# One bank table for eight PSUM banks, and a new order of steps, in a fused attention and transformer kernel

## The chip, the cores and the metric

The kernel is one program on one core of a Trainium2 chip. The metric is the device time of one execution in microseconds (us); less is better. Engines are named as in the profile: PE is TensorE (PEld its weight loads), DVE is VectorE, ACT is ScalarE, POOL is GpSimd and SP is SyncE, which here issues DMAs alone.

## The reference, cut to what matters

The input is x of shape 4 x 512 x 128 in float32. It goes through a small attention block and then through a six-layer transformer, each between layer norms and with a residual.

```python
x = x + layernorm(attention(layernorm(x)))        # 16 heads of 8, causal, rope, gelu on q and k
t = layernorm(x)
for i in range(6):                                # DEPTH
    s = shift_tokens(t)                           # features 64..127 moved down one token
    q, k, v = split(s @ Wqkv[i])                  # 16 heads of 64
    q, k = rotary(l2norm(q) * qs), rotary(l2norm(k) * ks)
    p = softmax(8 * q @ k.T)                      # windows of 32 tokens: own and previous
    t = (p @ v) @ Wo[i] + t
    s = shift_tokens(t)
    a, g = split((layernorm(s) * ln_g + ln_b) @ W1[i] + b1[i])
    t = (a * gelu(g)) @ W2[i] + b2[i] + t            # 341 hidden features
x = x + layernorm(t)
```

## The kernel before

There are two large stages. The first is the small attention block: 16 groups of four heads, each group 16 score steps that share four slots of two PSUM banks (`a_ring`) in turn. The loop of DVE there takes eight row maxima a group (L676), brings the output of the group two before into shape (`normalise`, L664 and L666, which reads a slot that PE wrote at L934), and adds the maxima to the queries (L682). PE waits for a slot until its last reader is done, so it waits for `normalise` before a later score step (L906) may write that slot.

The second stage is the transformer. A unit u is one layer of one of the four sequences, so there are 24 units. A unit is cut into steps, and each engine has a hand-kept table of steps (`TENSOR_STEPS`, `VECTOR_STEPS`, `SCALAR_STEPS`, `GPSIMD_STEPS`). A row (kind, n, lag) stands for step n of that kind of unit pass minus lag. `unrolled` runs the table once for each pass, so that in one pass an engine works on three or four units that are at different places. All engines execute in order; they meet by semaphores, one for each kind of step. The steps of a unit, with their lines:

- project 0 to 15: PE multiplies by one 128-column slice of Wk or Wq (L1003). DVE multiplies the result by cos and sin (rotate, L756), ACT squares it for the norms (L556). SP swaps neighbouring partitions by two DMAs (L428) and POOL adds the two halves (add, L490). The buffer between rotate and add has four slots, so rotate n waits for add n-4.
- sums 0 to 3: PE sums the squares (L1013), ACT copies the sums (nevac, L562), PE turns them (nturn, L1024), DVE takes inverse roots by Newton steps (newton, L768 and L712 to L723; for the keys also a split in three bf16 parts, L740 to L746).
- nback and spread: PE turns the keys' roots back (L1029), ACT copies them (nrows, L566), PE spreads them over the partitions (L1037), DVE multiplies the keys (keyed, L777).
- score 0 to 3: PE (L1056), mask and max on DVE (L781, L785), lower and scale on POOL (L494, L500), exp on ACT (L573), psum on DVE (L788, L790), pnorm on POOL (L504), flip on DVE (L794).
- xturn, mix and out: PE turns x (L1045), mixes it by the probabilities (L1072), ACT copies (zcopy, L578), PE multiplies by Wv Wo (out, L1080, made by the step vo at L980 once a layer) and ACT copies the sum (x1, L584 and L585).
- mean, var, rows, hid 0 to 2 and down: the feed-forward part on PE (L1090, L1096, L1101, L1110 and L1113, L1117), with center, xsq, bias, gelu and new on ACT and rstd, gain and gated on DVE.

PSUM has eight banks of 512 floats. In this stage they are three fixed groups: `ps_r` (two banks) for project, mean, var, rows, hid and down; `ps_s` (two) for sums 0 and 1, nturn 0, nback, spread, score and vo; `ps_z` (four) for mix, out, xturn, sums 2 and 3 and nturn 1. So project n takes the bank of project n-2 and waits until ACT has squared it, and score n waits until DVE has masked score n-1. Weights of the feed-forward part are loaded by SP in the middle of its swaps (`load_ffn`).

## Time and profile before

| what | value |
|---|---|
| device time, three runs | 2112.12, 2115.53, 2119.7 us; median 2115.53 |
| profiled execution, span from first to last instruction | 2110.2 us |
| busy: PE, DVE, POOL, ACT | 1875.9, 1560.5, 1102.0, 913.3 us |
| chain that ended last, by engine | PE 67%, DVE 21%, POOL 4%, waits of no known cause 3% |

The runs carry no split of time around the span; for the profiled execution the span is all that is known, and the median of the runs is 5.3 us longer. "Busy" of PE is modelled from the ends of matmuls, so its idle time is what is left between them. "Idle before" in a row is how long the engine had stood still ahead of that instruction, and the name behind the arrow is the instruction that released it. The mean time of one instruction on DVE in the page's table of groups is 1214 ns for the rotate at L756, 1220 for L781, 1211 for L785, 1209 for L788 and 1223 for L794.

### The profile page before, as it was taken

How to read it: one execution, taken by the hardware profiler on the slowest of the kernel's cores; microseconds unless marked ns; L12 is line 12 of the kernel's file. 1: busy time of each engine (PE TensorE's matmuls, PEld its weight loads, DVE VectorE, ACT ScalarE, POOL GpSimd, SP SyncE). 2: the span in 40 equal slices, each digit the busy share in tenths (PEclk: the TensorE clock that was granted, in tenths of full speed). 3: DMA queues.
4: the chain of work that ended last, by engine and by line, in shares of the span. 5: the costliest groups of instructions: out<-in, count | busy, mean ns of one | idle time of the engine just before them, and what ended most of it. 6: DMA issues, size and time to landing. Idle time of an engine off the chain costs nothing.

```text
span 2110.2 us, 47076 instructions
## 1 busy us (share of the span) xinstructions
PE 1875.9 (89%) x20040; PEld 812.5 (39%) x20040; DVE 1560.5 (74%) x2524; ACT 913.3 (43%) x1460; POOL 1102.0 (52%) x822
## 2 busy tenths in 40 slices
PE   5999956799999999999999999999999998999974
PEld 2333423344334433444344344333443344344421
DVE  5555557877887788778877877888778878787823
ACT  1344422334454444445444544444444444544531
POOL 2122213765576557655755675567546755675520
PEclk9899987889999999999999999999999999999987
DMA  2200001121311132112212212131113211221100
GB/s 57 81 12 11 1 1 72 69 79 49 115 71 47 53 104 93 64 52 76 94 54 86 81 61 74 59 120 61 49 54 110 86 57 62 80 72 46 57 0 20
DMA packets 91750, 131.42 MB, mean 62 GB/s; under 512 B 16242, under 2 KB 35856, under 8 KB 91536
## 3 DMA queue, kind: packets, MB, share of 16 engines
q1 hardware_dynamic: 91540, 128.41, 17.6%
q8 instruction: 157, 2.57, 0.5%
q14 instruction: 53, 0.43, 0.1%
HBM read 24.54 MB, written 1.05 MB: 12 GB/s over the span
## 4 chain that ended last, share of the span: by engine, by line
PE 67%; DVE 21%; POOL 4%; issue 3%; ACT 2%; DMA 2%; SPq 0%; POOLq 0%; DVEq 0%; ACTq 0%
PE ps_z L1080 15%; PE ps_r L1003 11%; PE ps_s L1056 7%; DVE t L756 6%; PE ps_r L1110 4%; PE ps_z L1072 3%; PE ps_r L1117 3%; PE ps_r L1113 3%; PE ps_z L1013 2%; DVE t L676 2%; POOL k_hat L490 2%; DVE n_tmp L718 2%; PE ps_z L888 2%; DVE rnorm L723 2%; DVE n_tmp L720 2%
## 5 line engine op out<-in xcount | busy, mean ns | idle before, releaser
L756 DVE TENSOR_TENSOR t<-ps_r,rot 128x1024 f32<-128x1024 f32 x384 | 457.8, 1214 | 143.2 <-PE ps_r L1003 136.6
L1003 PE MATMUL ps_r<-xs,w_qk_sb 128*128 128x512 f32 x768 | 436.0, 673 | 41.0 <-ACT sq L556 40.5
L556 ACT ACTIVATE sq<-ps_r 128x512 f32<-128x512 f32 x384 | 229.6, 598 | 353.0 <-DVE t L756 350.7
L490 POOL TENSOR_TENSOR q_hat<-t 128x512 f32<-128x512 f32 x192 | 241.9, 1272 | 210.8 <-DMA t<-t 210.3
L1080 PE MATMUL ps_z<-z,vo 128*128 128x512 f32 x768 | 350.1, 599 | 0.0
L494 POOL TENSOR_TENSOR prob<-prob,top 128x1024 f32<-128x1024 f32 x96 | 182.5, 1901 | 280.2 <-DVE top L785 280.1
L490 POOL TENSOR_TENSOR k_hat<-t 128x512 f32<-128x512 f32 x192 | 242.3, 1276 | 86.4 <-DMA t<-t 86.3
L1003 PEld LDWEIGHTS ps_r<-xs,w_qk_sb 128*128 128x128 f32 x768 | 130.7, 200 | 293.9 <-ACT sq L556 173.4
L504 POOL TENSOR_TENSOR prob<-prob,sinv 128x1024 f32<-128x1024 f32 x96 | 185.9, 1936 | 90.5 <-DVE sinv L790 90.5
L578 ACT ACTIVATE z<-ps_z 128x512 f32<-128x512 f32 x384 | 208.1, 603 | 36.1 <-PE ps_z L1072 35.9
L1080 PEld LDWEIGHTS ps_z<-z,vo 128*128 128x128 f32 x768 | 144.6, 191 | 180.0 <-issue 179.9
L1072 PE MATMUL ps_z<-pt,xtk 32*128 32x512 f32 x1536 | 196.9, 628 | 7.8 <-ACT z L578 6.5
L500 POOL TENSOR_TENSOR prob<-prob,rnorm 128x1024 f32<-128x1024 f32 x96 | 182.6, 1902 | 7.5 <-POOL prob L494 0.4
L480 POOL TENSOR_SCALAR_AFFINE_SELECT t<-t 128x256 f32<-128x256 f32 x128 | 51.9, 406 | 217.8 <-ACT t L535 217.6
L1056 PE MATMUL ps_s<-k_hat,q_hat 64*32 64x64 f32 x12288 | 151.5, 228 | 14.3 <-DVE prob L781 7.8
L1056 PEld LDWEIGHTS ps_s<-k_hat,q_hat 64*32 64x32 f32 x12288 | 131.2, 106 | 75.4 <-DVE prob L781 43.6
L781 DVE TENSOR_TENSOR prob<-ps_s,band 128x1024 f32<-128x1024 f32 x96 | 117.1, 1220 | 54.5 <-PE ps_s L1056 54.4
L777 DVE TENSOR_TENSOR k_hat<-k_hat,ps_s 128x1024 f32<-128x1024 f32 x96 | 116.5, 1213 | 30.6 <-PE ps_s L1037 30.6
L608 ACT ACTIVATE gate<-ps_r,vec 128x512 f32<-128x512 f32 (+1 forms) x72 | 49.4, 685 | 206.1 <-PE ps_r L1110 205.8
L788 DVE TENSOR_REDUCE sinv<-prob 128x16 f32<-128x1024 f32 x96 | 116.1, 1209 | 10.6 <-ACT prob L573 10.6
L794 DVE STREAM_TRANSPOSE pt<-prob 128x1024 f32<-128x1024 f32 x96 | 117.4, 1223 | 8.1 <-POOL prob L504 4.6
L1072 PEld LDWEIGHTS ps_z<-pt,xtk 32*128 32x128 f32 x1536 | 70.5, 187 | 127.2 <-ACT z L578 58.8
(188 smaller groups left out, 2560.4 us busy)
## 6 DMA issues: line engine op xcount, KB each, us to landing
t<-t SPq DMA_DIRECT2D x768, 128.0 KB, 2.0
rot<-in_dram SPq DMA_DIRECT2D x12, 512.0 KB, 4.8
w_qk_sb<-in_dram SPq DMA_DIRECT2D x24, 256.0 KB, 3.3
w_vt_sb<-in_dram SPq DMA_DIRECT2D x6, 512.0 KB, 4.7
w_o_sb<-in_dram SPq DMA_DIRECT2D x6, 512.0 KB, 5.8
z<-q_hat SPq DMA_DIRECT2D x128, 16.0 KB
w_sb<-in_dram SPq DMA_DIRECT2D x6, 341.0 KB
x_tok<-in_dram SPq DMA_DIRECT2D x4, 256.0 KB, 3.6
```

Of the source, the lines that this page charges most:

```text
L490: nc.gpsimd.tensor_tensor(dst, t12[:, slot, 0, :], t2[:, slot, :], ALU.add).then_inc(added.sem, 1)
L494: nc.gpsimd.tensor_tensor(s, s, top[:, (TT * u + n) % P_SLOTS, :].unsqueeze(2).to_broadcast([P, HEADS, 2 * WIN]), ALU.subtract).then_inc(l ...
L500: nc.gpsimd.tensor_tensor(s, s, by.unsqueeze(2).to_broadcast([P, HEADS, 2 * WIN]), ALU.mult).then_inc(scaled.sem, 1)
L504: nc.gpsimd.tensor_tensor(s, s, sinv[:, (TT * u + n) % P_SLOTS, :].unsqueeze(2).to_broadcast([P, HEADS, 2 * WIN]), ALU.mult).then_inc(p_no ...
L556: nc.scalar.activation(sq[:, n % SQ_SLOTS, :], ps_r[n % 2][:, :], ACT.Square).then_inc(squared.sem, 1)
L578: nc.scalar.activation(z[:, :, at:at + WIN], ps_z[:, w, :].rearrange("p (h n) -> p h n", n=WIN), ACT.Copy).then_inc(z_copied.sem, 1)
L756: nc.vector.tensor_tensor(t12[:, slot, :, :], ps_r[n % 2][:, :].unsqueeze(1).to_broadcast([P, 2, SEQ]), rot[:, n // PAIRS, :, :], ALU.mult ...
L794: nc.vector.transpose(pt[:, n % 2, :, :, :].rearrange("p h a n -> p (h a n)"), prob[:, (TT * u + n) % P_SLOTS, :, :, :].rearrange("p c e n ...
L1003: nc.tensor.matmul(ps_r[n % 2][:, :], w_qk_sb[:, n, :], xs[:, seq, WIN:WIN + SEQ], start=True, stop=True).then_inc(projected.sem, 1)
L1056: ins = nc.tensor.matmul(ps_s[WIN * w:WIN * (w + 1), e, 2 * WIN * c:2 * WIN * (c + 1)], q_hat[rows, pair_at(c), at:at + WIN], k_hat[rows, ...
L1072: ins = nc.tensor.matmul(ps_z[:, w, :], xtk[rows, a, n, :], pt[rows, n % 2, :, a, :], start=(a == 0), stop=(a == 1), skip_group_check=True)
L1080: ins = nc.tensor.matmul(ps_z[:, 0, :], vo[:, h, :], z[:, h, :], start=(h == 0), stop=False, skip_group_check=True)
```

## The change

Four things change.

1. All eight banks are one tensor `ps`. A table `BANKS` gives each step of a unit its bank or banks. A pass over PE's plan notes for each use of a bank who held it last (`before`), and `vacant` makes PE wait, ahead of the first matmul that writes a bank, for the reader of that last tenant. The old waits that stood for the fixed groups go.
2. All four tables of steps have another order and other lags. The passes are cut at another place; relative to project, the steps of a unit on PE have the same lag as before, but for xturn, out 0, mean and var, whose lag behind project is one pass less.
3. `load_ffn` is issued by ACT, right after the last new of a layer, and not by SP.
4. In the first stage, DVE's `normalise` stands ahead of the sixth maximum of a group and not behind it.

```diff
+BANKS = {
+    "project": [(1,), (3,), (7,), (2,), (5,), (3,), (1,), (2,), (7,), (0,), (5,), (1,), (4,), (0,), (3,), (5,)],
+    "score": [(0, 1), (5, 6), (2, 3), (0, 1)],
+    "mix": [(4, 3, 7, 6), (4, 0, 2, 3), (7, 4, 6, 0), (1, 5, 3, 2)],
...
-        ps_rr = ctx.enter_context(nc.psum_tensor("ps_r", [P, 2, 512], F32))
-        ps_s = ctx.enter_context(nc.psum_tensor("ps_s", [P, 2, 512], F32))
-        ps_z = ctx.enter_context(nc.psum_tensor("ps_z", [P, 4, 512], F32))
+        ps = ctx.enter_context(nc.psum_tensor("ps", [P, 8, 512], F32))
...
+        before, tenant = {}, {at: ("vo", 0, -1) for at in banks("vo")}
+        for kind, n, u in plan_pe:
...
+                        before[what, n // per, u, k] = tenant.get(at)
+                        tenant[at] = (what, n // per, u, k)
...
+            def vacant(what, n, u):
+                for k in range(len(banks(what, n))):
+                    held = before[what, n, u, k]
...
+                    if kind == "project":
+                        pe.wait_ge(squared.sem, squared.at(v, m))
...
+                    elif kind == "nturn":
+                        pe.wait_ge(n_newton.sem, n_newton.done(newton_at[v, m], 0))
...
                 if kind == "project":
...
-                    if n >= 2:
-                        pe.wait_ge(squared.sem, squared.at(u, n - 2))
-                    else:
-                        pe.wait_ge(squared.sem, squared.at(u - 1, 14 + n))
...
-                    nc.tensor.matmul(ps_r[n % 2][:, :], w_qk_sb[:, n, :], xs[:, seq, WIN:WIN + SEQ], start=True, stop=True).then_inc(projected.sem, 1)
+                    vacant("project", n, u)
+                    nc.tensor.matmul(ps[:, banks("project", n)[0], :], w_qk_sb[:, n, :], xs[:, seq, WIN:WIN + SEQ], start=True, stop=True).then_inc(projected.sem, 1)
...
-                if seq == 2 and c == 2 and layer:
-                    sp.wait_ge(x_new.sem, x_new.done(layer * BATCH - 1))
-                    load_ffn(layer)
...
+                    if seq == BATCH - 1 and layer + 1 < DEPTH:
+                        act.wait_ge(x_new.sem, x_new.done(u))
+                        load_ffn(layer + 1)
...
             for i in range(GROUPS + 2):
                 for n in range(A_STEPS):
+                    if n == OUT_AFTER + 1 and i >= 2:
+                        normalise(i - 2)
...
-                    if n == OUT_AFTER + 1 and i >= 2:
-                        normalise(i - 2)
```

Of the tables of steps the rows themselves are shown as they come out. On PE, in the middle of the transformer stage before the change, from nturn 0 (`ident,nsb`) over the mixes (`pt,xtk`) to nback (`ident_bf,rk_pad`) and the first spread (`rk_rows,sel_rows_bf`):

```order
L1024 MATMUL ps_s<-ident,nsb 128x128 x4
L1003 MATMUL ps_r<-xs,w_qk_sb 128x512
L1072 MATMUL ps_z<-pt,xtk 128x512 x8
L1003 MATMUL ps_r<-xs,w_qk_sb 128x512 x2
L1072 MATMUL ps_z<-pt,xtk 128x512 x8
L1029 MATMUL ps_s<-ident_bf,rk_pad 128x128 x4
L1037 MATMUL ps_s<-rk_rows,sel_rows_bf 128x512 x2
```

And now the same stretch, with the same right-hand names:

```order
L1086 MATMUL ps<-ident,nsb 128x128 x4
L1150 MATMUL ps<-x1s,centre_w 128x512
L1129 MATMUL ps<-pt,xtk 128x512 x16
L1107 MATMUL ps<-ident,xs 128x128 x4
L1072 MATMUL ps<-xs,w_qk_sb 128x512
L1107 MATMUL ps<-ident,xs 128x128 x4
L1072 MATMUL ps<-xs,w_qk_sb 128x512
L1092 MATMUL ps<-ident_bf,rk_pad 128x128 x4
L1072 MATMUL ps<-xs,w_qk_sb 128x512 x2
L1155 MATMUL ps<-mean_w,xsq 128x1 x4
L1139 MATMUL ps<-z,vo 128x512 x4
L1099 MATMUL ps<-rk_rows,sel_rows_bf 128x512 x4
```

Between nturn 0 and nback there stand now mean, mix 2 and 3, both xturn and two projects, where there stood three projects and two mixes; between nback and spread, where nothing stood, there are now two projects, var and out 0.

On ACT, in the middle of the transformer stage now, from the copies x1 (`x1s`) over the square of project 8 and the last exp of a unit (`prob`) to the copies of mix (`z`):

```order
L611 ACTIVATE x1s<-ps 64x512
L612 ACTIVATE x1s<-ps 64x512
L584 ACTIVATE sq<-ps 128x512
L599 ACTIVATE prob<-prob 128x1024
L588 ACTIVATE nsb<-ps 128x512
L605 ACTIVATE z<-ps 128x16x32 x2
```

The last exp of a unit stands now behind x1, which waits for out 3; before, x1 was earlier and the exp stood behind the copies of mix 0.

## Rows read from the trace of the kernel before

**Rows 1.** Page: busy us (share of the span) xinstructions.

```profile
PE 1875.9 (89%) x20040; PEld 812.5 (39%) x20040; DVE 1560.5 (74%) x2524; ACT 913.3 (43%) x1460; POOL 1102.0 (52%) x822
```

**Rows 2.** Stretches: length, busy us (instructions) by engine, granted clock, DMA share, GB/s.

```profile
118.00:281.00 163.00, 148.29 (x1409) 64.99 (x1407) 86.47 (x128) 72.20 (x105) 37.75 (x93) 0.95 0.04 8
329.00:518.00 189.00, 159.32 (x2051) 70.52 (x2052) 148.61 (x215) 70.95 (x118) 112.95 (x76) 0.87 0.21 74
518.00:1932.00 1414.00, 1328.69 (x14961) 571.63 (x14962) 1140.06 (x1752) 668.59 (x1082) 856.01 (x560) 0.98 0.21 73
```

**Rows 3.** Who waited for whom, PE, 518 to 1932 us: total, times, longest.

```profile
PE ps_s L1029 <- DVE rk_pad L746: 35.3, 20, 3.0
PE ps_r L1003 <- ACT sq L556: 28.7, 73, 1.5
PE ps_s L1037 <- ACT rk_rows L566: 13.8, 20, 0.7
PE ps_s L1056 <- issue: 5.1, 17, 0.9
```

**Rows 4.** One line's instructions: nback (durations ns, first and last start us).

```profile
L1029 PE MATMUL ps_s<-ident_bf,rk_pad x96: 219/219/314, 362.3 to 1970.2; 128*128 128x128 bf16 x96
```

**Rows 5.** PE in order of time: start, length, instruction, [idle before it].

```profile
1040.16 1.06 PE L1013 MATMUL ps_s<-sq,sel 128*32 128x512 f32 x8
...
1042.56 0.60 PE L1024 MATMUL ps_s<-ident,nsb 128*128 128x128 f32 x4
1043.00 1.02 PE L1003 MATMUL ps_r<-xs,w_qk_sb 128*128 128x512 f32 x2
...
1048.70 2.00 PE L1072 MATMUL ps_z<-pt,xtk 32*128 32x512 f32 x16
1052.42 0.40 PE L1029 MATMUL ps_s<-ident_bf,rk_pad 128*128 128x128 bf16 x4 [1.72 <-DVE rk_pad L746]
1053.51 0.39 PE L1037 MATMUL ps_s<-rk_rows,sel_rows_bf 32*128 32x512 bf16 x2 [0.69 <-ACT rk_rows L566]
1054.18 3.21 PE L1003 MATMUL ps_r<-xs,w_qk_sb 128*128 128x512 f32 x4 [0.28 <-ACT sq L556]
...
1063.67 3.70 PE L1080 MATMUL ps_z<-z,vo 128*128 128x512 f32 x8
```

**Rows 6.** DVE in order of time, from the rotates before newton 0.

```profile
1043.12 2.42 DVE L756 TENSOR_TENSOR t<-ps_r,rot 128x1024 f32<-128x1024 f32 x2
1045.45 0.21 DVE L768 TENSOR_SCALAR n_x<-ps_s 128x64 f32<-128x64 f32 x1
...
1047.05 1.27 DVE L718 TENSOR_TENSOR n_tmp<-rnorm 128x64 f32<-128x64 f32 x1
...
1049.86 0.23 DVE L718 TENSOR_TENSOR n_tmp<-rnorm 128x64 f32<-128x64 f32 x1
...
1052.14 0.23 DVE L746 TENSOR_TENSOR rk_pad<-n_tmp,rk_pad 128x64 bf16<-128x64 f32 x1
```

**Rows 7.** POOL in order of time, beside newton 0.

```profile
1046.95 2.54 POOL L490 TENSOR_TENSOR q_hat<-t 128x512 f32<-128x512 f32 x2 [0.21 <-DMA t<-t]
```

**Rows 8.** A stretch right after nback, columns as in Rows 2.

```profile
1055.10:1058.50 3.40, 3.40 (x9) 0.81 (x12) 2.79 (x3) 2.71 (x6) 2.31 (x2) 0.50 0.41 154
```

**Rows 9.** ACT in order of time: a copy x1, then the last exp.

```profile
1027.81 0.59 ACT L584 ACTIVATE x1s<-ps_z 64x512 f32<-64x512 f32 x1 [1.12 <-PE ps_z L987]
...
1035.97 1.06 ACT L573 ACTIVATE prob<-prob 128x1024 f32<-128x1024 f32 x1 [0.36 <-POOL prob L500]
```

**Rows 10.** SP in order of time: the first of four issues of load_ffn.

```profile
1027.24 0.58 SPq L407 DMA_DIRECT2D w_sb<-in_dram  x1
```

**Rows 11.** Who waited for whom, PE, 100 to 290 us.

```profile
PE ps_z L906 <- DVE k_hat L666: 6.0, 7, 0.9
PE ps_s L906 <- DVE k_hat L666: 5.1, 6, 0.9
```

**Rows 12.** Page, DMA issues: out<-in, count, KB each, median us to landing.

```profile
t<-t SPq DMA_DIRECT2D x768, 128.0 KB, 2.0
```

More of the change, by code:

```diff
@@ L73 @@
 TENSOR_STEPS = [
-    ("spread", 1, 1), ("sums", 2, 1), ("xturn", 0, 1), ("mean", 0, 3), ("xturn", 1, 1), ("spread", 2, 1),
-    ("sums", 3, 1), ("var", 0, 3), ("spread", 3, 1), ("out", 0, 2), ("rows", 0, 3), ("nturn", 1, 1), ("score", 0, 1),
-    ("hid", 0, 3), ("out", 1, 2), ("score", 1, 1), ("hid", 1, 3), ("score", 2, 1), ("hid", 2, 3), ("score", 3, 1),
-    ("down", 0, 3), ("project", 0, 0), ("out", 2, 2), ("project", 1, 0), ("project", 2, 0), ("out", 3, 2),
-    ("project", 3, 0), ("project", 4, 0), ("mix", 0, 1), ("project", 5, 0), ("vo", 0, 2), ("project", 6, 0),
@@ L79 @@
-    ("sums", 0, 0), ("project", 7, 0), ("mix", 1, 1), ("project", 8, 0), ("project", 9, 0), ("sums", 1, 0),
-    ("project", 10, 0), ("nturn", 0, 0), ("project", 11, 0), ("mix", 2, 1), ("project", 12, 0), ("project", 13, 0),
-    ("mix", 3, 1), ("nback", 0, 0), ("spread", 0, 0), ("project", 14, 0), ("project", 15, 0),
+    ("spread", 1, 3), ("sums", 2, 3), ("sums", 3, 3), ("rows", 0, 5), ("spread", 2, 3), ("spread", 3, 3),
+    ("nturn", 1, 3), ("out", 1, 4), ("hid", 0, 5), ("score", 0, 3), ("score", 1, 3), ("score", 2, 3),
@@ L82 @@
+    ("project", 13, 2), ("nback", 0, 2), ("project", 14, 2), ("project", 15, 2), ("var", 0, 4), ("out", 0, 3),
+    ("spread", 0, 2),
 ]
 VECTOR_STEPS = [
-    ("keyed", 0, 2), ("rotate", 14, 2), ("rotate", 15, 2), ("keyed", 1, 2), ("keyed", 2, 2), ("rstd", 0, 4),
-    ("keyed", 3, 2), ("gain", 0, 4), ("newton", 1, 2), ("mask", 0, 2), ("gated", 0, 4), ("max", 0, 2), ("mask", 1, 2),
-    ("max", 1, 2), ("gated", 1, 4), ("mask", 2, 2), ("gated", 2, 4), ("max", 2, 2), ("psum", 0, 2), ("rotate", 0, 1),
@@ L91 @@
+    ("psum", 0, 1), ("psum", 1, 1), ("rotate", 1, 0), ("flip", 0, 1), ("rotate", 2, 0),
 ]
 SCALAR_STEPS = [
[L93 to L96 removed]
@@ new lines @@
+    ("lower", 3, 4),
+]
+BANKS = {
+    "project": [(1,), (3,), (7,), (2,), (5,), (3,), (1,), (2,), (7,), (0,), (5,), (1,), (4,), (0,), (3,), (5,)],
+    "spread": [(6, 7), (2, 3), (6, 7), (0, 1)],
+    "score": [(0, 1), (5, 6), (2, 3), (0, 1)],
+    "vo": [(2, 3)],
+    "mix": [(4, 3, 7, 6), (4, 0, 2, 3), (7, 4, 6, 0), (1, 5, 3, 2)],
+    "sums": [(1,), (0,)],
+    "nturn": [(7,), (3,)],
+    "nback": [(6,)],
+    "xturn": [(7,), (1,)],
+    "out": [(4,)],
+    "mean": [(5,)],
+    "var": [(6,)],
+    "rows": [(5,)],
+    "gate": [(3,), (0,), (6,)],
+    "hid": [(7,), (5,), (0,)],
+    "down": [(6,)],
+}
@@ L112, in unrolled, with banks @@
+FILLS = {"hid": (("gate", 1), ("hid", 1)), "sums": (("sums", 2),), "out": (("out", 4),)}
+def banks(kind, n=0):
+    return BANKS[kind][n % len(BANKS[kind])]
 def unrolled(steps):
@@ L418, in _ @@
             load_vo(0)
-            load_ffn(0)
             move_heads(2)
```

234 lines of the change are left out of this document (132 added, 102 removed).

## The prediction, made before the changed kernel was run

> **What bounds the kernel now.** I read the page's busy shares first [rows 1]: PE is busy for 89% of the span, DVE for 74%, and nothing else is near. So PE is the engine to follow, and the question is what its idle 11% and its clock cost. Then the stretches [rows 2]. The transformer stage runs in a steady state from 518 to 1932 us, where PE is busy 1328.7 of 1414 us and idle 85.3 us. The pass length is read from nback, whose first and last matmul are 1607.9 us and 23 passes apart [rows 4]: 69.9 us a pass, so the steady stretch is about 20 passes, with 4.3 us of idle PE in each. Next, who made PE wait there [rows 3]: nback for DVE's newton and split 35.3 us, project for ACT's square 28.7 us, spread for ACT's copy of the turned roots 13.8 us, and 5.1 us without a known releaser. These four are 82.9 of the 85.3 us. All but the last are waits of the kind that a bank table and a new order can touch.
>
> The timeline shows one such place [rows 5]: nturn 0 starts at 1042.56, the last matmul before nback ends at 1050.70, then PE waits 1.72 us for DVE, then 0.69 for ACT, then 0.28 for a square. On DVE [rows 6] newton 0 could begin only at 1045.45 behind two rotates of 1.21 us, and ended with the split at 1052.37, so it took 6.9 us. Three of its small steps took near 1.2 us where the same form takes 0.23 later: the L718 at 1047.05 took 1.27 and the one at 1049.86 took 0.23. POOL's adds run until 1049.49 [rows 7], and the slow ones end with it.
>
> The clock is the last view. In the steady stretch PE was granted 0.98 of it. Right behind this stall the granted clock is 0.50 (1.2 instead of 2.4 GHz) with PE busy all the time [rows 8], and four matmuls of project take 3.21 us, where two take 1.02 [rows 5]. A mean of 0.98 over 1414 us is 28 us of lost work (21 to 35 with the rounding). So the pass is PE's work, about 64.7 us at full clock ((1328.7 - 28) / 20 = 65.0, or 64.3 with the pass of 69.9), plus 4.3 us of waits and 1.4 us of clock.
>
> **The change part by part.** No matmul is added or taken away, so the work of a pass stays at 65 us. What changes is what lies beside it.
>
> Project for square, 28.7 us. With two banks in turn, project n waits for square n-2, which waits for rotate n-2. In the new table no project comes back to its bank sooner than four projects later (0 and 6 share bank 1, 1 and 5 bank 3), and most of PE's other steps stand between. With PE's durations [rows 5] (project 0.95 in a row, mix and score 1.9 or less, a quarter of out 3.4 to 3.7) project 5 is some 5 us behind project 1, in whose time rotate and square (1.2 and 0.6) fit four times. I take 0.1 a pass for what is left; bounds 0 and 1.4, as now.
>
> nback for newton, 35.3 us. Between the end of nturn 0 and nback PE does now mean, two mixes of 2.00, two xturn like the nturn of 0.60, and two projects of 1.02 [rows 5]; mean has a project's shape and so its time. That is 1.02 + 4.00 + 1.20 + 2.04 = 8.3 us, less 0.1 for each overlap, 7.8 us. Before, it was three projects and two mixes, 6.9 us of work. Newton takes 6.9 us with POOL at work beside it. So it hides if DVE begins it within 0.9 us of the end of nturn 0; before, it began 2.3 us late. In the new DVE order newton 0 stands behind flip 3, and what leads to that is a chain: out 3 on PE, the two copies x1 of 0.59 each, a square, the last exp of 1.06 [rows 9], then psum 3, flip 2, two rotates and flip 3 on DVE, five of about 1.2 us (the rotate's, [rows 6]) and a reciprocal. A square takes as long as such a copy. From the end of out 3 that is 1.2 + 0.6 + 1.1 + 6.3 = 9.2 us. PE does in the same time the two sums, mix 0, two projects, mix 1 and nturn 0: 2.1 + 2.0 + 2.0 + 2.0 + 0.6, less overlaps, 8.2 us. So DVE begins newton 1.0 us late, which just does not fit the 0.9. I take 0.4 us of wait a pass at mix 2 (it needs the bank that newton 0's first step reads) and 0.3 at nback; bounds 0 and 2 us together (the present 1.8).
>
> spread for the copy, 13.8 us. The copy of 0.69 us lies now beside two projects, var and out 0, over 6 us [rows 5]. It goes wholly: 0; upper bound the present 0.7.
>
> New waits. mix 0 now needs the bank of out (so x1) and of project 8 (so its square, which ACT does behind x1): 1.8 us of ACT behind out 3 against the 1.9 us of two sums. mix 3 and xturn 1 need banks whose readers stand close ahead. Queued behind a waiting mix on PE is all of PE. I take 0.2 for these, bounds 0 and 1, and leave the 0.25 without releaser. In sum 0.1 + 0.7 + 0.2 + 0.25 = about 1.2 us a pass instead of 4.3. On 20 passes: 85.3 - 24 = 61 us saved.
>
> Clock. Without the row of waits at nback, PE's longest pause in a pass is under half a microsecond. I take that 24 of the 28 us come back; bounds 0 and 28.
>
> The rule that speaks against this is in the Trainium skill, "TensorE: Matmul & The Clock Gate", section "A second HAM failure mode: psum-queue depth-cycling": cycling through PSUM banks makes PE pause briefly and often, so that the clock swings between its levels. Here PE pauses less with more banks and the dip stands behind the one long stall; by that rule the clock would fall more often, and the result is the third rival.
>
> First passes of the stage. From 329 to 518 us PE is idle 29.7 us at a clock of 0.87 [rows 2]. In the first unit there is nothing to fill in, so its norm chain stays bare. Only the projects' waits go. I take 8 us, bounds 0 and 20. The last units, from 1932 us on, are a bare chain too: 0, bounds -6 and +6.
>
> normalise put ahead. PE waited 13 times, 11.1 us in all, for `normalise` at the score step that takes its slot [rows 11], because DVE first did a maximum that waits for a later matmul. The turned output is ready one step sooner on PE, so DVE has it done by the time PE comes. The maximum itself comes no later, since it waits for PE anyway. PE is busy 148.3 of 163 us there [rows 2], so it is what bounds: 11 us, bounds 0 and 12.
>
> load_ffn on ACT. Four issues of at most 0.58 us [rows 10] are 2.3 us, five times, in ACT's queue. Behind them stand the squares of projects 6 and 7, which are needed by sums 1 over 8 us later, and ACT is busy 47% [rows 2]. SP gets them off its swaps. I take 0, bounds -12 (all bare) and +5.
>
> The sum: 61 + 24 + 8 + 0 + 11 + 0 = 104 us. The span 2110.2 becomes 2006; with the 5.3 us by which the median of the runs is above the span, 2011.5 us. I forecast 2012.
>
> **The rivals.**
>
> Newton stays late. POOL and DVE pull on each other: if POOL has more adds to do while newton 0 runs, more of its 17 steps take 1.2 instead of 0.23, and each costs 1.0 us. The trace shows three such steps. The Trainium skill ("SBUF — State Buffer", "Who interferes with whom") says that a DVE instruction with two SBUF inputs and a GpSimd instruction that reads SBUF shut each other out; the row agrees, with 1.27 against 0.23. If three more are hit, nback waits as long as now and the clock dips as now, and only the projects' waits (28 us), the spread's copy (14), the first passes and normalise go: 28 + 14 + 8 + 11 = 61, so 2055.
>
> DVE becomes the bound, and it is slower than before. DVE is busy 1140.1 of 1414 us, 57 us a pass [rows 2]. A rotate waits for the add four before it. The swap between them takes two issues of some 0.6 us and 2.0 us to land [rows 12, 10], and the add 1.27 [rows 7]; with the rotate's 1.2 the round is 5.7 us for four rotates, 1.4 each. POOL's new order puts scale 3 and pnorm 2 between adds 5 and 6 and pnorm 3 behind add 7, 1.9 us each. If the 13 rotates behind mask 3 each lost 1.2 us, DVE would need 57 + 16 = 73 us a pass, over the 70.7 of now: 24 x 2.3 = 55 us more, less 11 of normalise, so 2160. It decides from 13.7 us of new waits of DVE on; below that it costs nothing up to the PE pass of 66. For it: DVE has one queue and now 9 us of slack, not 14. Against it: POOL is busy 42.8 us a pass, and its extra steps lie where DVE has masks and flips to do.
>
> The clock swings with the banks. If a dip like that of [rows 8] came twice a pass, each 3.4 us at half speed, it would cost 3.4 instead of 1.4 us a pass. The waits still go: 61 + 8 + 11 - 24 x 2.0 = 32, so 2084. Against it, every part of the present loss that I see stands behind the one stall.
>
> Nothing moves. PE's ends are modelled, and if its idle time were not real, removing it gains nothing but normalise: 2104 or, within 0.3% of 2115.5, no change. Against it, the waits have their releasers by name.
>
> **How the numbers follow.** The forecast 0.66, newton late 0.20, DVE the bound 0.07, clock 0.03, nothing 0.04. A change of less than 0.3% can't be told from none here. Faster takes the first two and the clock, less a little for mishaps: 0.88. The same: 0.04. Slower 0.08. The range: if all waits and dips go and every lower bound holds, it is 85 + 28 + 20 + 12 + 6 = 151 us, or 1964; I stop at 1975, since some wait always stays. Upward it takes in newton late (2055) with some 15 us for the unknown ends: 2070.
>
> **What would show it.** In the profile after: passes of 66 us between nbacks; no wait over 0.5 us of nback or spread; PE's idle under 30 us in 20 passes; the granted clock near 1.0 in the steady stretch; no PE wait for L703 (the old L666). DVE should be busy over 85% there. Wrong would be: DVE waiting for POOL's adds in each pass, newton steps of 1.2 us in number, or PE waits of a microsecond at mix 0 or mix 2, which would say that ACT's order (x1 ahead of the last exp) is what ends last.

## The result: 1.4% faster, and the profile after

The changed kernel takes 2085.57 us (median of 4 runs, 2077.06 to 2092.18), against 2115.64 (2112.12 to 2119.7, 4 runs) for the kernel before. The ratio is 0.9862, with a 95% interval of 0.9824 to 0.9899. So it is faster by 30 us, where I forecast 104, and the time lies above my range of 1975 to 2070. The profiled execution took 2084.88 us, its span is 2083.2 us, 27 less than before.

The busy shares of the page after, to set beside [rows 1]:

```profile
PE 1820.3 (87%) x20040; PEld 843.8 (41%) x20040; DVE 1601.3 (77%) x2524; ACT 911.0 (44%) x1460; POOL 1096.4 (53%) x822
```

PE is still the engine that bounds, with less busy time than before. The stretches show where the span's 27 us come from. Columns as in [rows 2]: us, busy of PE, PEld, DVE, ACT and POOL, then granted clock, DMA share and GB/s. First the kernel before, from the first `normalise` of the first stage to its last:

```profile
93.00:289.00 196.00, 177.73 (x1686) 78.05 (x1684) 101.71 (x151) 87.83 (x130) 46.64 (x115) 0.95 0.03 7
```

The kernel after: the first stage, the steady stretch (from the first down to the 21st of 24, 20 passes, as before), and a piece of one pass.

```profile
91.00:263.00 172.00, 163.54 (x1690) 71.99 (x1690) 102.45 (x150) 88.35 (x130) 46.65 (x115) 1.00 0.04 7
...
493.50:1923.80 1430.30, 1304.29 (x14962) 606.48 (x14961) 1175.83 (x1752) 665.48 (x1080) 850.87 (x561) 0.94 0.21 72
...
1546.70:1553.50 6.80, 5.48 (x33) 2.54 (x34) 1.38 (x2) 0.69 (x1) 5.27 (x3) 0.50 0.01 2
```

The first stage gains 24 us, where I had 11. Its first `normalise` also stands 2.9 us earlier (90.4 us, before 93.3), and the first passes behind the stage lose 2 (230.7 us from the last `normalise` to the first down, before 228.8), so the first down stands 24.3 us earlier. The steady stretch runs between the same two downs in both kernels (after 493.52 and 1923.77, before 517.86 and 1931.55). It takes 1430.3 us instead of 1413.7: it is **16.6 us slower**, 71.5 us a pass instead of 70.7. PE is busy 24 us less in it, but idle 126.0 us instead of 85.3, and the granted clock is 0.94 instead of 0.98. The rest comes from the end. From that 21st down to the end it is 178.7 us before (2110.2 - 1931.5) and 159.4 after (2083.2 - 1923.8). That is 19 us, where I had put 0. It belongs to the new tables of steps: every run with them has 157 to 163 us there, every run with the old ones 179. The likely reason is that xturn, out 0, mean and var of a unit stand one pass sooner; no run moves these alone. Together -24.3 + 16.6 - 19.3 = -27.0.

Who makes PE wait in the steady stretch after (line, releaser, us in total, times, longest):

```profile
PE ps L1118 <- issue: 72.4, 36, 2.5
PE ps L1161 <- DVE v_rstd L760: 22.2, 18, 1.6
PE ps L1086 <- DVE k_hat L814: 14.5, 20, 0.7
PE ps L1099 <- DVE k_hat L814: 9.7, 20, 0.5
...
PE ps L1072 <- ACT sq L584: 1.4, 2, 1.1
```

Of the waits of [rows 3], project for square went from 28.7 to 1.4 us, and nback for newton and spread for ACT's copy are gone from the list. Two new groups are in their place. 72.4 us stand ahead of score (L1118) with the releaser "issue", that is, PE waited for no other engine that the profile shows. 46.4 us stand ahead of rows, nturn 1 and spread 2, behind DVE's rstd.

The timeline of PE in one pass shows the first group (start, duration, line, tile, shape and count, in brackets the idle time ahead):

```profile
1540.19 2.45 PE L1118 MATMUL ps<-k_hat,q_hat 64*32 64x64 f32 x229
1544.53 1.47 PE L1118 MATMUL ps<-k_hat,q_hat 64*32 64x64 f32 x128 [1.90 <-issue]
1548.02 0.67 PE L1118 MATMUL ps<-k_hat,q_hat 64*32 64x64 f32 x27 [2.02 <-issue]
1548.62 2.07 PE L1072 MATMUL ps<-xs,w_qk_sb 128*128 128x512 f32 x2
```

Three score steps stand in a row in the new order (384 matmuls). The first 229 run in 2.45 us, then PE pauses 1.90, does exactly 128 in 1.47, pauses 2.02, and does the last 27. The two project matmuls behind it take 2.07 us instead of 1.02, and the stretch from 1546.7 is at 0.50 of the clock (1.2 instead of 2.4 GHz) for 6.8 us. The pauses have a counterpart among the DMAs of these 10 us, on queue q8, which carries instructions:

```profile
q8 instruction: 3, 0.05, 1.8%
```

Three packets, 0.05 MB, so 16 KB each, at 1542.15, 1545.58 and 1549.12: one each 3.5 us. A score step of 128 matmuls has 128 weight loads too, 256 instructions. Over the whole program the page has 158 such packets for 20040 + 20040 instructions of PE, also about 256 a packet. So by this reading a score step uses up a whole packet of instructions in 1.4 us, while the packets come 3.5 us apart. In no trace of this case do two packets of q8 stand less than 3.26 us apart.

The second group, on PE and then on DVE and POOL:

```profile
1530.50 0.65 PE L1161 MATMUL ps<-ident,v_rstd 128*128 128x128 f32 x4 [1.10 <-DVE v_rstd L760]
1531.63 0.39 PE L1099 MATMUL ps<-rk_rows,sel_rows_bf 32*128 32x512 bf16 x4 [0.48 <-DVE k_hat L814]
1532.76 0.90 PE L1086 MATMUL ps<-ident,nsb 128*128 128x128 f32 x4 [0.73 <-DVE k_hat L814]
```

```profile
1524.68 0.15 DVE L836 TENSOR_SCALAR v_sum<-ps 128x4 f32<-128x4 f32 x1
...
1525.38 1.24 DVE L751 TENSOR_SCALAR v_rstd<-v_rstd 128x4 int32<-128x4 int32 x1
...
1526.86 1.18 DVE L757 TENSOR_TENSOR v_tmp<-v_tmp,v_half 128x4 f32<-128x4 f32 x1
...
1528.86 1.19 DVE L755 TENSOR_TENSOR v_tmp<-v_rstd 128x4 f32<-128x4 f32 x1
1530.08 0.16 DVE L757 TENSOR_TENSOR v_tmp<-v_tmp,v_half 128x4 f32<-128x4 f32 x1
```

```profile
1524.05 3.96 POOL L518 TENSOR_TENSOR q_hat<-t 128x512 f32<-128x512 f32 x3 [7.18 <-DMA t<-t]
1528.76 1.27 POOL L518 TENSOR_TENSOR q_hat<-t 128x512 f32<-128x512 f32 x1 [0.74 <-DMA t<-t]
```

The rstd of the norm takes 5.7 us, from 1524.68 to 1530.4. In the pass before the change that I looked at (1063.45 to 1065.8) it takes 2.3, with no step over 0.17. Three of its steps take 1.2 us now, all while POOL adds. It is so in the whole run: all 24 rstds took 2.3 us before, 22 of 24 take 4.6 to 5.9 us now, and each of their 86 steps of over 0.3 us lies beside an instruction of POOL. POOL worked for at most 0.3 us of an rstd before, and works for 3.3 to 4.6 us of each of these 22 now (the last two, with POOL idle, take 2.3). DVE also begins 1.0 us behind the end of var, with four rotates ahead. PE has 5.7 us of work between var and rows (out 0, spread 1, sums 2 and 3), and 1.0 + 5.7 us is more than that. rows waits for it, and spread 2 and nturn 1 wait for the keyed steps that DVE does behind it, 2.3 us a pass together.

### The profile page after: what moved, and what is told of

The parts are those of the page before. It is cut to its first block, busy times and chain, and to the rows that moved or that the text cites. A ratio compares the mean times of both kernels' runs of the same rounds, so it can differ in the third digit from the quotient of the medians.

```text
span 2083.2 us, 47244 instructions
## 1 busy us (share of the span) xinstructions
PE 1820.3 (87%) x20040; PEld 843.8 (41%) x20040; DVE 1601.3 (77%) x2524; ACT 911.0 (44%) x1460; POOL 1096.4 (53%) x822
## 4 chain that ended last, share of the span: by engine, by line
PE 62%; DVE 25%; issue 8%; POOL 3%; ACT 1%; DMA 0%; POOLq 0%; SPq 0%; DVEq 0%; ACTq 0%
PE ps L1139 13%; PE ps L1072 12%; PE ps L1118 6%; PE ps L1129 5%; DVE t L793 4%; PE ps L1169 4%; PE ps L925 3%; PE ps L1171 3%; PE ps L1177 3%; DVE k_hat L814 3%; PE ps L1062 2%; PE ps L1079 2%; DVE t L715 2%; PE ps L954 2%; DVE v_tmp L755 2%
## 5 line engine op out<-in xcount | busy, mean ns | idle before, releaser
L793 DVE TENSOR_TENSOR t<-ps,rot 128x1024 f32<-128x1024 f32 x384 | 447.8, 1205 | 13.1 <-PE ps L1072 10.5
L1072 PE MATMUL ps<-xs,w_qk_sb 128*128 128x512 f32 x768 | 397.0, 640 | 8.5 <-ACT sq L584 4.2
L1139 PE MATMUL ps<-z,vo 128*128 128x512 f32 x768 | 373.4, 632 | 1.4 <-ACT z L605 1.4
L584 ACT ACTIVATE sq<-ps 128x512 f32<-128x512 f32 x384 | 229.7, 600 | 243.2 <-DVE t L793 238.9
L1139 PEld LDWEIGHTS ps<-z,vo 128*128 128x128 f32 x768 | 153.4, 206 | 181.4 <-issue 179.0
L1118 PE MATMUL ps<-k_hat,q_hat 64*32 64x64 f32 x12288 | 149.9, 236 | 86.7 <-issue 85.6
L605 ACT ACTIVATE z<-ps 128x512 f32<-128x512 f32 x384 | 203.9, 609 | 31.6 <-PE ps L1129 31.5
L1072 PEld LDWEIGHTS ps<-xs,w_qk_sb 128*128 128x128 f32 x768 | 136.9, 197 | 162.8 <-issue 139.0
L1129 PE MATMUL ps<-pt,xtk 32*128 32x512 f32 x1536 | 187.2, 612 | 7.6 <-DVE n_x L805 1.5
L1118 PEld LDWEIGHTS ps<-k_hat,q_hat 64*32 64x32 f32 x12288 | 133.3, 110 | 129.8 <-issue 126.8
```

The lines of the kernel that those rows point to most:

```text
L584: nc.scalar.activation(sq[:, n % SQ_SLOTS, :], ps[:, banks("project", n)[0], :], ACT.Square).then_inc(squared.sem, 1)
L605: nc.scalar.activation(z[:, :, at:at + WIN], ps[:, banks("mix", t)[w], :].rearrange("p (h n) -> p h n", n=WIN), ACT.Copy).then_inc(z_copie ...
L793: nc.vector.tensor_tensor(t12[:, slot, :, :], ps[:, banks("project", n)[0], :].unsqueeze(1).to_broadcast([P, 2, SEQ]), rot[:, n // PAIRS, ...
L1072: nc.tensor.matmul(ps[:, banks("project", n)[0], :], w_qk_sb[:, n, :], xs[:, seq, WIN:WIN + SEQ], start=True, stop=True).then_inc(projecte ...
L1118: ins = nc.tensor.matmul(ps[WIN * w:WIN * (w + 1), banks("score", n)[e], 2 * WIN * c:2 * WIN * (c + 1)], q_hat[rows, pair_at(c), at:at + W ...
L1129: ins = nc.tensor.matmul(ps[:, banks("mix", n)[w], :], xtk[rows, a, n, :], pt[rows, n % 2, :, a, :], start=(a == 0), stop=(a == 1), skip_g ...
```

## The experiments

Ratios are to the kernel before, with their 95% intervals. Steps that a diff calls by name are rows of PE's table of steps, `("kind", number, lag)`, or entries of `BANKS`.

**Scores apart.** In the changed kernel, other steps stand between the scores; two banks change with it.

```diff
-    ("nturn", 1, 3), ("out", 1, 4), ("hid", 0, 5), ("score", 0, 3), ("score", 1, 3), ("score", 2, 3),
-    ("project", 0, 2), ("hid", 1, 5), ("hid", 2, 5), ("out", 2, 4), ("project", 1, 2), ("project", 2, 2),
+    ("nturn", 1, 3), ("out", 1, 4), ("hid", 0, 5), ("score", 0, 3), ("out", 2, 4), ("score", 1, 3),
+    ("hid", 1, 5), ("score", 2, 3), ("project", 0, 2), ("hid", 2, 5), ("project", 1, 2), ("project", 2, 2),
```

> The changed kernel with PE's table altered in one place: out 2 stands between score 0 and score 1, hid 1 between score 1 and score 2, and hid 2 behind project 0; project 0 and the second half of hid 1 exchange banks 5 and 1, so that no new bank wait arises. Same instructions. Theory (three score steps in a row, 384 small matmuls, run out of fetched instructions; in the changed kernel PE stands 72.4 us without a releaser in 20 passes and the clock drops behind it): the waits without releaser fall under 10 us in 20 passes, the long dip of the clock behind them goes, and the pass falls from 71.5 by 3.6 us of idle and 2 to 3 of clock to about 65.5 us; time about 1955 to 1985. Rival (these are waits for DVE's masks that the profile does not name, or the price of many small matmuls wherever they stand): idle of the score steps stays near 3.7 us a pass and the time at 2075 to 2095.

It took 2025.67 us, ratio 0.9569 (0.9530 to 0.9607): 60 us less than the changed kernel. Its waits of PE in the steady stretch, and the stretch itself:

```profile
PE ps L1072 <- ACT sq L584: 36.3, 21, 1.9
PE ps L1161 <- DVE v_rstd L760: 22.9, 19, 2.0
...
PE ps L1118 <- issue: 0.7, 2, 0.4
```

```profile
492.80:1864.60 1371.80, 1281.29 (x14961) 586.64 (x14960) 1178.73 (x1751) 666.05 (x1080) 852.92 (x561) 0.97 0.22 75
```

The wait at score is gone (72.4 to 0.7 us) and the clock is up from 0.94 to 0.97. So the row of scores is the cause of that wait. The gain is smaller than I expected (1955 to 1985 us), because a new wait took part of it: project 5 shares bank 3 with project 1 and now comes sooner behind it, so it waits 36.3 us in all for project 1's square.

**Small matmuls in a row.** To see whether the pause is of the instructions or of the score's data, a piece is put at the very end of the changed kernel: four blocks of 512 small matmuls of the score's shape, with 64, 128, 256 and again 64 columns, and 24 wide matmuls behind each block. Its time is read from the trace alone; the kernel took 2200.01 us with the piece in it.

```diff
+            for cols in (64, 128, 256, 64):
+                for j in range(256):
...
+                    nc.tensor.matmul(ps[WIN * (j % 4):WIN * (j % 4 + 1), j // 4 % 2, 0:cols], q_hat[0:64, j % 8, at:at + WIN],
+                                     k_hat[0:64, j % 8, WIN + at:WIN + at + cols], start=True, stop=True)
```

> The changed kernel with an extra piece at the end of the layer stage, whose results nothing reads: four blocks of 256 matmul calls (512 matmul and 512 weight-load instructions each) in a row on 64x32 tiles without any semaphore between, of 64, 128, 256 and again 64 columns, each followed by 12 wide matmul calls. Theory (instruction fetch is the limit: a score step of 128 matmuls in a row takes 1.4 us alone and 3.5 us when it follows another): the 64-column blocks show pauses of about 2 us after each 128 matmuls, some 3.5 us per 128; the 128-column block is paced by the same fetch, at 3.5 us per 128 too; the 256-column block, whose matmuls last longer, shows shorter pauses or none. Rival (PE waited for DVE in the score steps): no pauses in any block, since nothing is waited for here. The whole adds 40 to 80 us.

```profile
2061.16 13.24 PE L1188 MATMUL ps<-k_hat,q_hat 64*32 64x64 f32 x512 [1.48 <-ACT xs L630]
...
2087.12 14.18 PE L1188 MATMUL ps<-k_hat,q_hat 64*32 64x128 f32 x512
...
2111.72 27.83 PE L1188 MATMUL ps<-k_hat,q_hat 64*32 64x256 f32 x512
...
2149.98 2.47 PE L1188 MATMUL ps<-k_hat,q_hat 64*32 64x64 f32 x161
2153.76 3.40 PE L1188 MATMUL ps<-k_hat,q_hat 64*32 64x64 f32 x128 [1.31 <-issue]
2157.51 3.63 PE L1188 MATMUL ps<-k_hat,q_hat 64*32 64x64 f32 x128 [0.34 <-issue]
```

The last block, small again, runs its first 161 matmuls at full clock, and then it has a pause of 1.31 us and further ones behind pieces of 128. Its packets of instructions come at 2151.11, 2155.24 and 2159.23. But from the first pause on the granted clock is 0.50 to 0.55, as here (columns as in [rows 2]):

```profile
2157.50:2161.10 3.60, 3.60 (x128) 3.43 (x128) 0.00 (x0) 0.00 (x0) 0.00 (x0) 0.50 0.02 5
```

So the 3.75 to 4.0 us from one piece of 128 to the next are mostly the matmuls themselves at half clock. The 128-column block takes 14.18 / 4 = 3.5 us for each 128 matmuls at full clock and never pauses, nor does the 256-column one, nor the first 64-column block, which ran at half clock (0.53) and took 3.3 us for 128. I had expected pauses of about 2 us in both 64-column blocks. What this piece shows is that PE pauses in a long row of small matmuls with no other engine and no score to wait for, and that the same row pauses less or not at all when it goes slower. Since it has one pause at full clock, it gives the edge only roughly.

**Rate or row.** The same piece with blocks of 128 small matmuls and 4, 3, 2 or 1 wide calls (two matmuls each) between them tells a limit on the rate from a limit on how many small ones stand in a row.

```diff
+            for wide in (4, 3, 2, 1):
...
+                for block in range(5):
+                    for j in range(64):
...
+                    for h in range(wide):
+                        nc.tensor.matmul(ps[:, 3, :], vo[:, h, :], z[:, h, :], start=True, stop=True)
```

> The changed kernel with an extra piece at its end, whose results nothing reads: five blocks of 128 small matmuls (64 columns, as a score step), each followed by 4, then 3, 2 and 1 wide matmul calls (two instructions of 512 columns each, 0.9 us a call), without semaphores between. Theory (a block of 128 small matmuls and as many weight loads is one 16 KB instruction DMA, and such a DMA comes each 3.5 us at best): with 4 and 3 calls (1.4 + 3.5 and 1.4 + 2.6 us) there is no pause, with 2 calls (1.4 + 1.7 = 3.1) a pause of 0.2 to 0.6 us a block, with 1 call one of 1.0 to 1.5. Rival (the pause belongs to a number of matmuls in a row, not to a rate): with one wide call between them the pauses are gone too.

```profile
2164.53 1.99 PE L1191 MATMUL ps<-k_hat,q_hat 64*32 64x64 f32 x128
2166.45 1.98 PE L1194 MATMUL ps<-z,vo 128*128 128x512 f32 x4
...
2184.81 0.85 PE L1191 MATMUL ps<-k_hat,q_hat 64*32 64x64 f32 x43
2185.88 1.42 PE L1191 MATMUL ps<-k_hat,q_hat 64*32 64x64 f32 x85 [0.21 <-issue]
...
2189.62 1.43 PE L1191 MATMUL ps<-k_hat,q_hat 64*32 64x64 f32 x87 [0.54 <-issue]
```

The granted clock is 1.00 in all of these blocks. With two wide calls a block and its filling take 3.8 us and nothing pauses; with one, where they would take 3.1 us, the pauses come and fill it up to about 3.5 (3.47, 3.75 and 3.39 us from block to block). So it is a rate, and about 3.5 us for each 256 instructions is the edge. My expectations of a pause with two calls and of one of 1.0 to 1.5 us with one call missed, since the small block takes 1.99 us here and not the 1.4 of a score. (The kernel took 2218.98 us with its piece.)

**out 1 first.** For the second new wait: in the changed kernel, out 1 goes ahead of rows, to give rstd time.

```diff
-    ("spread", 1, 3), ("sums", 2, 3), ("sums", 3, 3), ("rows", 0, 5), ("spread", 2, 3), ("spread", 3, 3),
-    ("nturn", 1, 3), ("out", 1, 4), ("hid", 0, 5), ("score", 0, 3), ("score", 1, 3), ("score", 2, 3),
+    ("spread", 1, 3), ("sums", 2, 3), ("sums", 3, 3), ("out", 1, 4), ("rows", 0, 5), ("spread", 2, 3), ("spread", 3, 3),
+    ("nturn", 1, 3), ("hid", 0, 5), ("score", 0, 3), ("score", 1, 3), ("score", 2, 3),
```

> The changed kernel with out 1 moved ahead of rows on PE, nothing else. In the changed kernel rows waits 22.2 us in 20 passes for DVE's rstd, and nturn 1 and spread another 24.2 for DVE's keyed behind it. Theory (DVE is late with rstd, and 3.4 us of out 1 would cover it): these waits fall from 46 to under 10 us, but hid 0 comes sooner behind gain and bias and may wait up to 2 us a pass; net 0 to 30 us faster, 2055 to 2085. Rival (DVE's lateness only moves on to hid 0): waits of hid 0 of 2 us a pass, no gain, 2075 to 2095. The three scores in a row stay, so their 72 us of waits without releaser should be unchanged by either.

2091.81 us, ratio 0.9887 (0.9837 to 0.9937), not to be told from the changed kernel. Its waits of PE:

```profile
PE ps L1118 <- issue: 70.2, 36, 2.5
PE ps L1169 <- DVE n_x L805: 54.8, 20, 2.7
```

The waits at rows, spread and nturn are gone and hid 0 (L1169) waits instead, 2.7 us a pass, for DVE's first step of newton 1: gate 0 is the first half of the step hid 0 and uses bank 3, which nturn 1 held, and nothing stands between the two any more. That is the rival that I had named, the lateness only moves on. So order and bank table have to be changed together.

**Project 5 later.** The scores apart as above, with project 5 behind down.

```diff
-    ("score", 3, 3), ("project", 3, 2), ("project", 4, 2), ("project", 5, 2), ("down", 0, 5), ("project", 6, 2),
+    ("score", 3, 3), ("project", 3, 2), ("project", 4, 2), ("down", 0, 5), ("project", 5, 2), ("project", 6, 2),
```

> The kernel with the score steps apart (e1_scores_apart), and project 5 behind down instead of ahead of it. In that kernel project 5 waited 36.3 us in 20 passes for the square of project 1, whose bank it takes, since DVE reaches rotate 1 later there. Theory (down's 3.7 us cover the wait, and the waits of rows, nturn 1 and spread, 47 us in 20 passes, stay): PE's waits fall by 30 to 36 us, some clock with them, time 1975 to 2000. Rival (DVE is late anyway and the wait comes back at a later bank or at mix): 2015 to 2035.

2006.28 us, ratio 0.9511 (0.9468 to 0.9554), 6 us above the range that I expected. The wait for square fell from 36.3 to 11.0 us, the steady stretch from 1371.8 to 1352.2, at a clock of 0.98:

```profile
PE ps L1161 <- DVE v_rstd L760: 25.4, 17, 1.6
PE ps L1072 <- ACT sq L584: 11.0, 19, 0.6
```

**normalise, one way and the other.** First the kernel before with `normalise` put ahead and nothing else:

```diff
                 for n in range(A_STEPS):
+                    if n == OUT_AFTER + 1 and i >= 2:
+                        normalise(i - 2)
...
-                    if n == OUT_AFTER + 1 and i >= 2:
-                        normalise(i - 2)
```

> The kernel before with one part of the change alone: normalise ahead of the sixth maximum. Theory: the 11 us that PE waits for it in the first stage go, 2104 (2102 to 2107), and nothing else in the profile changes. Rival (another wait takes its place, since DVE then does the maximum later): 2112 to 2118.

2082.88 us, ratio 0.9835 (0.9796 to 0.9875), where I expected 2104: these two lines alone gain as much as the whole change. Its stretches:

```profile
91.00:263.00 172.00, 163.96 (x1698) 72.10 (x1696) 103.05 (x152) 88.34 (x130) 47.04 (x116) 1.00 0.04 7
491.20:1904.80 1413.60, 1327.47 (x14972) 570.10 (x14961) 1139.74 (x1751) 668.35 (x1081) 855.98 (x560) 0.98 0.21 73
```

The first stage is that of the changed kernel, the steady stretch is that of before to a tenth of a microsecond. Then the changed kernel with `normalise` behind the maximum again (the same diff, the other way round):

> The changed kernel with normalise behind the sixth maximum again, as before the change. Theory (normalise alone brings 25 us in the first stage, by the two traces, and the layer stage brings next to nothing): 2108 to 2118, the time of the kernel before. Rival (the table of banks and the new order carry a good part of the gain): 2085 to 2100.

2113.51 us (10 runs), ratio 1.0014 (0.9984 to 1.0045). Without `normalise`, the rest of the change nets nothing. Here the same 14 pauses of 0.85 us cost more than before the change: from the first `normalise` to the last it is 204.8 us at a clock of 0.90, in the kernel before 195.8 at 0.95, and with `normalise` ahead 172.4 at 1.00 in either kernel.

**load_ffn on SP again**, in the changed kernel:

```diff
+                if seq == 2 and c == 2 and layer:
+                    sp.wait_ge(x_new.sem, x_new.done(layer * BATCH - 1))
+                    load_ffn(layer)
...
-                    if seq == BATCH - 1 and layer + 1 < DEPTH:
-                        act.wait_ge(x_new.sem, x_new.done(u))
-                        load_ffn(layer + 1)
```

> The changed kernel with load_ffn issued by SP in the middle of its swaps again. Theory (this part of the change is hidden on either engine): within 6 us of the changed kernel, 2080 to 2092. Rival (four issues of up to 0.6 us in ACT's queue delay squares, or on SP delay swaps, and PE waits for them): 10 us or more away on either side.

2100.56 us (10 runs), ratio 0.9962 (0.9937 to 0.9987), a span of 2096.6, 13.4 more than the changed kernel (9 us of it in the steady stretch, 4 ahead of it). That is not the nothing I expected, but the rival of 10 us or more. One row of its waits of PE is new:

```profile
PE ps L1079 <- ACT sq L594: 13.2, 5, 2.8
```

Once a layer sums wait, 2.6 us on average, for a square. In the trace SP sits at its wait for the last new of the layer until 1579.2, then issues four transfers of 0.35 to 0.44 us, and the swaps queue behind all that. Then **the kernel before with `normalise` ahead and load_ffn on ACT**, to see whether it is worth as much in the old order:

> The kernel before with two parts of the change: normalise ahead (as e4_before_norm, 2083) and load_ffn issued by ACT. Theory (in the new order load_ffn on SP cost 15 us more than on ACT, since SP's four issues and its wait hold up swaps in five passes, and sums then wait up to 2.8 us for a square): it costs something in the old order as well, 2068 to 2080, and then the banks and the new order by themselves make the kernel slower by 5 to 17 us. Rival (only the new order, in which sums stand close behind the squares, is held up by the swaps): 2080 to 2086, and the three parts do not add up.

2088.61 us (5 runs), ratio 0.9910 (0.9878 to 0.9942), against 2082.88 with `normalise` alone: no gain, and perhaps a small loss. It lies above both ranges that I had named (2068 to 2080, rival 2080 to 2086). Its PE waits are the old ones:

```profile
PE ps_r L1003 <- ACT sq L546: 37.5, 77, 2.3
PE ps_s L1029 <- DVE rk_pad L746: 33.4, 20, 3.0
```

I read this as slack that the swaps had at that place in the old order and lack in the new one; no run measures the slack itself. What is shown is that the parts of this change don't simply add up.

**A new table.** With all this, a version of the changed kernel: out 1 ahead of rows and out 2 ahead of hid 0 (fills the time of rstd and of newton 1), hid 1 and 2 between the scores, project 5 behind down, banks to match, and on DVE gated 0 and 1 each behind its own mask.

```diff
+    ("spread", 1, 3), ("sums", 2, 3), ("sums", 3, 3), ("out", 1, 4), ("rows", 0, 5), ("spread", 2, 3), ("spread", 3, 3),
+    ("nturn", 1, 3), ("out", 2, 4), ("hid", 0, 5), ("score", 0, 3), ("hid", 1, 5), ("score", 1, 3), ("hid", 2, 5),
+    ("score", 2, 3), ("project", 0, 2), ("project", 1, 2), ("project", 2, 2), ("score", 3, 3), ("project", 3, 2),
+    ("project", 4, 2), ("down", 0, 5), ("project", 5, 2), ("project", 6, 2),
...
+    "project": [(6,), (2,), (3,), (7,), (6,), (2,), (1,), (3,), (7,), (0,), (5,), (1,), (4,), (0,), (3,), (5,)],
...
+    "score": [(0, 1), (2, 3), (0, 1), (0, 1)],
...
+    "gate": [(2,), (5,), (7,)],
+    "hid": [(7,), (6,), (5,)],
+    "down": [(5,)],
```

> The changed kernel with another table for PE: out 1 ahead of rows and out 2 ahead of hid 0, hid 1 and hid 2 between the score steps, project 5 behind down; the banks of project 0 to 7, score 1 and 2, gate, hid and down altered so that none comes back while its reader is late; on DVE gated 0 and 1 each behind their mask. It takes away all three causes at once: score steps in a row (72 us in 20 passes in the changed kernel), rows, nturn 1 and spread behind DVE's rstd (46 us), and project 5 (36 us in e1). Theory (these are the causes, with the clock's drops behind them): idle PE under 2 us a pass, the clock near 1.0, a pass of 63 to 65 us, time 1930 to 1960. Rival (DVE, busy 58 to 60 us a pass, becomes the bound once PE no longer waits, so that nback or mix wait): a pass of 67 or more, time 1990 to 2020.

1963.45 us (1960.02 to 1973.01), ratio 0.9297 (0.9250 to 0.9343): 7% faster than before, the best version found, and 3 us above the 1930 to 1960 that I expected. Its steady stretch and its largest waits of PE:

```profile
489.20:1808.60 1319.40, 1258.30 (x14962) 575.19 (x14961) 1198.41 (x1752) 670.33 (x1080) 850.37 (x562) 0.99 0.22 78
```

```profile
PE ps L1129 <- issue: 19.1, 16, 7.9
PE ps L1072 <- DVE prob L818: 13.7, 19, 1.8
PE ps L1129 <- DVE n_x L805: 8.9, 14, 1.1
```

66.0 us a pass, PE idle 61 us in 20 passes, clock 0.99. rstd still has three steps of 1.2 us in the pass I looked at, but out 1 covers them. 13 of the 20 passes take 63.8 to 65.7 us. The longest, 72.4 us, has the one pause of 7.9 us at a mix, which is 0.4% of the time. Its releaser "issue" hides a chain that starts at DVE:

```profile
568.04 8.00 DVE L766 TENSOR_SCALAR rot<-rot,qk_scale_sb 128x1024 f32<-128x1024 f32 x1
```

```profile
578.02 3.79 PE L1129 MATMUL ps<-pt,xtk 32*128 32x512 f32 x16 [7.93 <-issue]
```

This step scales the table for the rotates of the queries. It takes 0.66 to 1.9 us each other time in the two kernels and this version, and here 8.00, while POOL works without a gap from 565.60 to 575.48; it ends 0.56 us behind POOL. Then come the rotate of project 8 (576.07), its square (577.33 to 577.93) and the mix, which needs that bank.

## Why the prediction was wrong, point by point

**The waits that I said would go, went.** project for square: 28.7 to 1.4 us (I said 2). nback and mix 2 for newton: 35.3 to nothing in the list (I said 14). The row behind it is DVE's: newton 0 now begins at 1514.09 and ends at 1520.2, and nback starts at 1520.73 with no wait. It began 0.65 us behind the end of nturn 0 (1513.44), where I had 1.0, and newton took 6.1 us and not 6.9; PE's work between nturn 0 and nback was 7.3 us, where I had 7.8. spread for the copy: 13.8 to nothing. These three waits gave back 76 us, where the sum had 61 for all waits, new ones included.

**The step that failed is "new waits ... 0.2 for these".** I looked for new waits only at the banks of mix and xturn, and never asked of each moved step what PE itself needs to issue it. I had a row that pointed to it: the wait of score with releaser "issue", 5.1 us in [rows 3], which I left as it was. With three scores in a row it became 72.4 us. Before, wide steps stood between the scores. Taken apart, 72.4 became 0.7 us and the kernel 60 us faster, and the two pieces at the end pause without any of the kernel's work around them, the second at an edge of 3.5 us.

**The clock went the other way.** I took 24 us back from it, and it fell from 0.98 to 0.94. In the 20 passes the clock falls to 0.50 15 times before the change, for 68 us in all, and 34 times after it, for 173 us: 18 times behind the pauses at score, as in the 6.8 us shown above, and 16 times behind the wait for rstd (4 us from 1533 at 0.57). At half speed that is up to 87 us of lost work instead of 34, where I had 28 for the kernel before. This is my third rival by its price (2084, the result is 2086), but not by its cause. The rule that I weighed there (the Trainium skill, "TensorE: Matmul & The Clock Gate", "A second HAM failure mode: psum-queue depth-cycling") puts such pauses down to the turn through the banks. The version with the new table turns through the same eight banks and has a clock of 0.99, with three falls in 20 passes, so here it is the pauses at score and rstd, and not the banks. That the price agrees is chance: in that rival the waits of PE would have fallen by 61 us, and they rose by 41.

**rstd was not in my sum.** I named steps of 1.2 us for newton, as the rival "newton stays late". The mechanism is right and hit the other Newton chain of the same code: rstd takes 5.7 instead of 2.3 us, begins 1.0 us late, and PE's work up to rows covers only 5.7 us of that. The waits at rows, nturn 1 and spread 2 are 46 us. That POOL is the cause is read from the timelines, in which all 86 slow steps lie beside POOL; no run took POOL's adds away. They agree with the rule I cited on DVE and GpSimd (the Trainium skill, "SBUF — State Buffer", "Who interferes with whom") by 1.2 us against 0.16, but not all are of the kind that I named there: 39 of the 86 (L749, L751 and L752) have one SBUF input, not two. What is shown is that these waits come from DVE being behind: with 3.4 us of out 1 in between they are gone and stand at the next thing that DVE has to deliver, newton 1, instead. How much of the lateness is the slow steps and how much the order on DVE, no run takes apart.

**normalise** was mis-sized: 24 us in the first stage and 31 in the run by itself, where I had 11 with 12 as an upper bound. I priced only the idle time of PE in [rows 11]. Two groups take 26.52 us before (L906 at 161.68 and 188.20) and 24.27 after (L925 at 163.94 and 188.21), 1.12 less each, of which 0.85 is the wait. The rest lies in these rows, of before and of after:

```profile
186.86 0.49 PE L888 MATMUL ps_r<-z 32*128 32x128 f32 x4
188.20 0.49 PE L906 MATMUL ps_z<-xc,z 32*128 32x128 f32 x4 [0.85 <-DVE k_hat L666]
```

```profile
188.21 0.38 PE L925 MATMUL ps<-z 32*128 32x128 f32 x2
188.22 0.38 PE L943 MATMUL ps<-xsq,z 32*128 32x128 f32 x2
```

The two lines run side by side on two row tiles of 32, and the wait between them pulled them apart. The granted clock is 1.00 between the two points in both kernels. 13 groups of 1.12 are 14.6 us. The other 9 are the clock of the whole stage, 0.95 before and 1.00 after on 178 us of work. I had read [rows 2] of that stage for its idle time only.

**load_ffn**: I said 0, with -12 as the end of the range where all is bare. It is worth 15 us by the medians (13 by the spans) in the new order and nothing in the old one. I looked at ACT's queue, where the issues came, and not long enough at SP's, from which they went: there a wait goes too, and swaps stand behind it.

**The tail and the first passes**: the tail 19 us for my 0, since I took the end for a bare chain and did not ask what it means that four kinds of its steps are now one pass sooner. The first passes lost 2 us where I had a gain of 8. (The 151 us of my lower end also leave out the 5 us that I had allowed load_ffn; that decides nothing here.)

**DVE as the bound** did not come. It is busy 82% of the steady stretch (my sign was 85%), and 91% in the best version, and its waits stayed small.

The steady stretch is what the forecast missed: I had it 85 us shorter, and it is 17 longer. That the whole still came out 30 us faster is luck as far as the prediction goes: the first stage and the tail gave 43 us, where I had 11. In sum, by the two traces: -24 first stage, -19 tail, +17 steady stretch, where the old waits gave back about 76 us and PE's work some, and the new ones (72 at score, 46 behind rstd) and the clock took more. My "work of a pass stays at 65 us" did not hold either: 1304.3 x 0.94 is 1226, or 61.3 us a pass at full clock, and in the best version 1258.3 x 0.99 gives 62.3 (the rounding of the clock is 0.3 us a pass). No matmul is gone, so PE's steps overlap more in the new order, or their modelled ends do. Two mixes in a row take 3.71 us where two apart take 2.00 each; that is the smaller part. By tile, at the granted clock of each stretch, 26 us of the 20 passes are in project (315 to 289 us) and 11 in spread (26 to 14), two of the steps that stood behind waits before the change; why they read shorter stays open.

## What to carry to other kernels

Before steps are put in a new order, look at what each asks of the engine's own instruction stream: here PE had to have 3.5 us of work for each 256 instructions, and rows of small matmuls need wide ones between them. An "issue" wait in the list before is a price for each such step, not a rest to be carried over. Price a wait by what it pulls apart and by the clock of its whole stage, and where an issue is moved away, look at the queue that it leaves as closely as at the one that it joins.
